# Later loading of one weight half, column-tiled bias product and shared moments in the prologue of a two-layer graph kernel

## Chip, cores and metric

The kernel runs as one program on one core of one Trainium2 chip. The metric is the device time of one execution in microseconds (us). The engines that matter here are TensorE (PE, matmuls and transposes), VectorE (DVE), ScalarE (ACT), GpSimd (POOL) and the DMA engines, which SyncE (SP) and ACT feed. Each engine works through its own instructions in order, so that an instruction that waits holds up all that stands behind it.

## What is computed

There are 1250 nodes with 512 features each and 40,000 edges with a source, a target and a row of 512 attributes. Cut to what matters:

```
h  = relu(layernorm(x))
msg = (h[src] + edge_attr) @ Wm.T + bm           # 40000 x 512
agg = segment_sum(msg, dst) / max(degree, 1)
upd = concat(h, agg) @ Wu.T + bu                 # Wu is 512 x 1024
x  = x + layernorm(h + gelu(upd)) * gamma + beta
h  = relu(layernorm(x))
x  = x + (relu(((1 + eps) * h + segment_sum(h[src], dst)) @ W1 + b1) @ W2 + b2) + h
```

## The kernel before

The edge attributes are 82 MB and are read once. They come in 79 groups of 512 edges (1 MB each), and one loop, `for n in range(NG)`, stands on every engine; "group n" below is one turn of it. Three kinds of work lie in a group on PE:

- `sums(n)` (line 1091; line 1099 from group 59 on) multiplies a one-hot matrix of targets (`oneD`) with the group's rows (`ea`) in 4 slots. ACT copies the result out (`packed_copy`, line 481), PE transposes it (`turn`, line 1119), ACT copies that out (`turned_copy`, line 487, two buffers `turned_sums`), and POOL adds it to `aggT` (`add_sums_of`, line 422, two additions for a group). Since there are two buffers, `turned_copy(n)` waits from n = 2 on for POOL's additions of group n - 2 (semaphore `early_step`).
- `counts(m)` (line 1110) multiplies one-hot matrices of sources and keys (`oneS`, `oneK`, line 675 on DVE), and DVE adds the result to the table of counts `A16` in two halves (line 696). The counts run ahead: groups 0, 3, 6, ... have two, the others one, until all are done in group 58 (`FULL`). `counts(m)` waits for the additions of counts m - 2.
- One piece of other work may stand at the end of a group (`ASIDE`): a transpose of four 128x128 blocks of h (`T_AT`, line 1132), the first quarter of a product h times Wu's first half (`U_AT`, line 1137; the other three quarters stand in later groups), or, in groups 0 and 1, a product of the prologue. They write PSUM banks 6 and 7 in turn, and each waits until the one two places before it has been copied out (`bank_free`).

Ahead of the loop stands a prologue. Wu is 512 x 1024; its second half (`Wu2T`) is needed for the products CT = Wm.T times Wu2.T (line 1054), its first half (`Wu1T`) only for the quarters of line 1137. PE transposes all eight block columns (line 1036), makes product 0, transposes the tables of indices (line 1061), and makes products 1 and 2. Product 3 stands in group 0, and the product of the bias bm with Wu2 in group 1, as four matmuls whose stationary operand `bmB` is bm broadcast to 128 columns.

x's moments: DVE takes `bn_stats` of seven of ten row blocks before the loop and of three in group 0 (line 777), aggregates them (line 782) and writes `ve` (line 784). POOL raises it to the power -1/2 (line 408). This instruction stands on POOL ahead of all its additions of line 422. DVE makes `nb0` of it in group 2 (line 827), and ACT writes h block by block from group 2 on (`H0_AT`, line 492).

The DMA queue of SP holds, in order: indices, Wu's first half, Wm, edge groups 0 and 1, x, bm, edge groups 2 and 3, bu; then edge group n + 4 after `sums(n)`. ACT's queue holds Wu's second half in two parts. After group 58, `Hh` takes h's high part (line 504), `A16` is converted in pieces (line 515), and from group 60 on PE multiplies them (lines 1190 and 1191).

## Time and profile before

| | us |
|---|---|
| median of 3 runs (lowest to highest) | 490.38 (489.9 to 492.35) |
| profiled execution, its own time | 489.93 |
| its span, first to last instruction | 488.1 |
| PE busy | 472.6, 97% of the span |
| DVE, ACT, POOL busy | 269.4, 158.0, 122.2 |

The span is cut into stretches by reading when `sums(n)` starts: `sums(0)` at 25.91 us, `sums(5)` at 43.70, `sums(8)` at 51.40, `sums(48)` at 158.82 and `sums(60)` at 188.68. Idle time of an engine costs something only where another one waits for it in the end; PE is the engine to watch.

### The profile page before, as it was taken

The numbers are of one execution on the slowest core, as the hardware profiler recorded it, in microseconds if no ns is written. First come the engines' busy times: TensorE is split into PE (matmuls) and PEld (weight loads), VectorE is DVE, ScalarE is ACT, GpSimd is POOL, SyncE is SP. The second block draws the span as 40 slices with busy tenths as digits, with TensorE's granted clock in tenths as the row PEclk, the third lists the DMA queues.
The fourth block names the chain that finished last, engine by engine and source line by source line (L and its number), as shares of the span: only waits on it lengthen the run. The fifth ranks groups of instructions, "written<-read, shape, count | busy, mean of one in ns | idle before, by whom it ended". The sixth has DMA issues, their size and how long they took to land.

```text
span 488.1 us, 9290 instructions
## 1 busy us (share of the span) xinstructions
PE 472.6 (97%) x3275; PEld 277.4 (57%) x3275; DVE 269.4 (55%) x621; ACT 158.0 (32%) x291; POOL 122.2 (25%) x183
## 2 busy tenths in 40 slices
PE   4999999999999999999999999899999999999997
PEld 3545555555555446776766655699744449444442
DVE  4789878787878887977857699923000000011011
ACT  6726633332333327411047287620012123000000
POOL 4005433444343432000001113349990000000000
PEclk9899999999999999999999999999999999999999
DMA  8998999999999999999430111040130000010111
GB/s 297 381 351 282 410 389 395 398 407 401 396 391 397 397 401 405 401 339 299 147 109 24 43 30 53 0 173 1 45 128 1 0 0 1 21 43 21 44 43 38
DMA packets 31641, 98.92 MB, mean 203 GB/s; under 512 B 3593, under 2 KB 4617, under 8 KB 31595
## 3 DMA queue, kind: packets, MB, share of 16 engines
q1 hardware_dynamic: 30458, 97.27, 53.1%
q10 hardware_dynamic: 1136, 1.05, 0.7%
q8 instruction: 27, 0.44, 0.4%
q14 instruction: 20, 0.16, 0.1%
HBM read 95.76 MB, written 2.56 MB: 201 GB/s over the span
## 4 chain that ended last, share of the span: by engine, by line
PE 81%; DVE 10%; DMA 4%; issue 3%; SPq 1%; POOL 1%; DVEq 0%; POOLq 0%
PE ps L1355 14%; PE ps L1340 14%; PE ps L1091 10%; PE ps L1137 7%; PE ps L1110 6%; PE ps L1190 6%; PE ps L1191 5%; PE ps L1287 4%; PE ps L1099 4%; DMA X<-in_x_dram 4%; PE ps L1119 4%; PE ps L1263 3%; PE ps L1264 3%; DVE A L696 2%; DVE stats L777 1%
## 5 line engine op out<-in xcount | busy, mean ns | idle before, releaser
L422 POOL TENSOR_TENSOR aggT<-turned_sums,aggT 128x88 f32 x118 | 62.5, 530 | 88.1 <-ACT turned_sums L487 74.8
L1025 DVE TENSOR_TENSOR U<-ps,U 128x512 f32<-128x512 f32 (+1 forms) x10 | 6.9, 693 | 128.5 <-PE ps L1355 128.5
L696 DVE TENSOR_TENSOR A<-ps,A 128x220 f32 x158 | 60.7, 384 | 28.6 <-PE ps L1110 18.0
L1355 PE MATMUL ps<-W2s,hid 128*128 128x512 f32 (+1 forms) x160 | 68.8, 592 | 0.0
L1340 PE MATMUL ps<-aggT,W1s 128*128 (+1 forms) x192 | 67.3, 513 | 0.0
L1091 PE MATMUL ps<-ea,oneD 128*22 128x256 f32 x944 | 62.7, 383 | 0.0
L1340 PEld LDWEIGHTS ps<-aggT,W1s 128*128 128x128 f32 x192 | 36.4, 190 | 30.7 <-issue 30.6
L1355 PEld LDWEIGHTS ps<-W2s,hid 128*128 128x128 f32 (+1 forms) x160 | 30.0, 188 | 38.2 <-issue 38.2
L481 ACT COPY packed_sums<-ps 128x256 f32<-128x256 f32 x59 | 22.0, 372 | 90.4 <-PE ps L1091 90.4
L1091 PEld LDWEIGHTS ps<-ea,oneD 128*22 128x22 f32 x944 | 22.6, 101 | 46.5 <-issue 21.7
L1263 PE MATMUL ps<-AR,Hh 128*128 128x256 f32 (+2 forms) x160 | 44.0, 311 | 0.7 <-DVE Hl L992 0.7
L1264 PE MATMUL ps<-AR,Hl 128*128 128x256 f32 (+2 forms) x160 | 43.0, 306 | 0.0
L1110 PE MATMUL ps<-oneK,oneS 128*128 128x220 bf16 x316 | 41.2, 260 | 1.7 <-DVE A L696 1.5
L675 DVE TENSOR_TENSOR oneK<-iotaP,P_key 128x1760 bf16<-128x1760 bf16 (+1 forms) x40 | 42.3, 1057 | 0.0
L1137 PE MATMUL ps<-Wu1T,U 128*128 128x512 f32 x80 | 41.3, 598 | 0.0
L605 ACT ACTIVATE hid<-ps,b1C 128x512 f32 (+1 forms) x24 | 14.6, 608 | 77.7 <-PE ps L1340 77.7
L432 POOL TENSOR_TENSOR rs<-ve,mhalf 128x1 f32<-128x1 f32 x10 | 8.3, 829 | 113.1 <-DVE ve L957 113.1
L1287 PE MATMUL ps<-CT,aggT 128*128 128x512 f32 x80 | 35.7, 592 | 0.0
L1190 PE MATMUL ps<-ARc,Hh 128*128 128x512 f32 x80 | 33.8, 423 | 0.0
L1110 PEld LDWEIGHTS ps<-oneK,oneS 128*128 128x128 bf16 x316 | 29.7, 97 | 5.0 <-DVE oneK L675 2.2
L1263 PEld LDWEIGHTS ps<-AR,Hh 128*128 128x128 f32 x160 | 30.2, 189 | 2.7 <-DVE Hl L992 1.1
L1191 PE MATMUL ps<-ARc,Hl 128*128 128x512 f32 x80 | 31.6, 394 | 0.0
(133 smaller groups left out, 642.7 us busy)
## 6 DMA issues: line engine op xcount, KB each, us to landing
ea<-in_edge_attr_dram SPq DMA_DIRECT2D x78, 1024.0 KB, 7.8
X<-in_x_dram SPq DMA_DIRECT2D x1, 2304.0 KB
xt<-in_x_dram SPq DMA_DIRECT2D x9, 256.0 KB, 3.5
out_dram<-U SPq DMA_DIRECT2D x9, 256.0 KB
W1s<-in_L_gnn_W_dram SPq DMA_DIRECT2D x1, 2048.0 KB, 9.1
W2s<-in_L_gnn_W_dram SPq DMA_DIRECT2D x1, 2048.0 KB, 8.5
WuN<-in_L_gnn_Wu_dram ACTq DMA_DIRECT2D x2, 512.0 KB, 4.4
WuN<-in_L_gnn_Wu_dram SPq DMA_DIRECT2D x1, 1024.0 KB, 6.8
```

Source lines behind the costliest of these rows:

```text
L422: nc.gpsimd.tensor_tensor(cols, sums, cols, ALU.add).then_inc(early_step, 1)
L696: V.tensor_tensor(cols, ps[:, 4 + m % 2, half * KW:(half + 1) * KW].rearrange("p (h w) -> p h w", w=W), cols, ALU.add).then_inc(add_step, 1)
L1091: last = T.matmul(to.rearrange("p (c d) -> p c d", c=2), oneD[h][:, g * 2 + j, :], data, start=j == 0, stop=j == 1)
L1110: last = T.matmul(ps[:, 4 + m % 2, (j // 2) * KW:(j // 2 + 1) * KW], sources[:, j // 2, :, j % 2], keys[:, j // 2, :, j % 2], start=j % 2 ...
L1137: quarter = T.matmul(ps[:, ASIDE_BANK["u1", b], :], U[:, b, f * P:(f + 1) * P], Wu1T[:, f, :], start=f == 0, stop=f == FC - 1)
L1190: T.matmul(to, Hh[:, c, rows], here, start=c == 0 and (q < 2 or f % 2 == 0), stop=False)
L1191: last = T.matmul(to, Hl[:, c, rows], here, start=False, stop=c == NT - 1 and (q < 2 or f % 2 == 1))
L1263: T.matmul(to, Hh[:, b, rows], AR[:, b, start:start + cols], start=b == 0 and (cols == 512 or f % 2 == 0), stop=False)
L1264: last = T.matmul(to, Hl[:, b, rows], AR[:, b, start:start + cols], start=False, stop=b == NT - 1 and (cols == 512 or f % 2 == 1))
L1287: last = T.matmul(ps[:, 2 + b % 2, :], aggT[:, f, b * P:(b + 1) * P], CT[:, f, :], start=f == 0, stop=f == FC - 1)
L1340: last = T.matmul(ps[:, CHUNK_BANK[k % 4], 0:cols], W1s[:, f, k * P:(k + 1) * P], aggT[:, f, bass.ds(start, cols)], start=f == 0, stop=f = ...
L1355: last = T.matmul(ps[0:rows, 6 + b % 2, :], hid[:, k, b * P:b * P + rows], W2s[:, k, :], start=k == 0, stop=k == KC - 1)
```

## The change

- The DMA of Wu's first half (now its own tile `Wu1N`) goes behind x in SP's queue; its four transposes move from the prologue into groups 2 to 5, with their copies on ACT.
- The prologue's order on PE is: four transposes of Wu's second half, products 0 and 1, the tables of indices, product 2. Product 3 is cut in two halves, in groups 0 and 1.
- The bias product is made in groups 57 and 58: four matmuls that write 32 rows each (column tiles, line `bias_parts`), a copy, and one matmul with a matrix of ones that adds the four. `Wu2T` and `WmN` have to live until then, so they lie in `Hh`, and `high_h0(0)` waits for the end of the bias product.
- DVE takes the moments of row blocks 0 to 4 only, in groups 0 and 1. Blocks 5 to 9 are ACT's: five ACTIVATEs that write the row sum with `accum_out` in group 0, five that square x minus the mean with `accum_out` in group 2. DVE makes the means in group 1 and `ve` in group 3; `nb0` moves to group 4, and h's blocks (`H0_AT`) from groups 2 to 11 to groups 5 to 14.
- h's transposes move from groups 4, 5, 6, 9, 15, ... 45 to 6, 7, 9, 15, ... 45, 48; the quarters start in group 8, not 7, and one of them stands in group 54.
- The least indices of targets (`offs`) are written and sent first, and the zeroing of `aggT` on ACT stands ahead of `A16`'s second half; the sum of uncovered edges is taken in group 6.

```diff
-    MOMENTS = 7
+    MOMENTS = [(0, 3), (3, 5)]
+    BY_ACT = slice(5, NT)
-    H0_AT = list(range(2, 2 + NT))
-    T_AT = [4, 5, 6] + list(range(9, 9 + 6 * (NT - 3), 6))
-    QUARTERS = [n for n in range(7, FULL) if len(COUNTS[n]) == 1 or (n % 6 == 0 and 6 < n < 48)]
+    LATE_PRODUCT_AT = [0, 1]
+    WU1_AT = [2, 3, 4, 5]
+    BIAS_PRODUCT_AT = [FULL - 1, FULL]
+    H0_AT = list(range(5, 5 + NT))
+    T_AT = [6, 7, 9] + list(range(15, 15 + 6 * (NT - 4), 6)) + [48]
+    QUARTERS = [n for n in range(8, FULL) if len(COUNTS[n]) == 1 or (n % 6 == 0 and n not in T_AT)]
...
-            sp.dma_start(WuN[:, :, 0:D], Wu[:, 0:D].rearrange("(o p) i -> p o i", p=P)).then_inc(wu1_in, 16)
             sp.dma_start(WmN[:], Wm.rearrange("(m p) i -> p m i", p=P)).then_inc(wm_in, 16)
...
                     sp.dma_start(X[0:TAIL, NT - 1, :], x[(NT - 1) * P:N, :]).then_inc(x_in, 16)
+                    sp.dma_start(Wu1N[:], Wu[:, 0:D].rearrange("(o p) i -> p o i", p=P)).then_inc(wu1_in, 16)
...
+            def sums_of_x():
+                act.wait_ge(x_in, 32)
+                for b in range(*BY_ACT.indices(NT)):
+                    nc.scalar.activation(U[:, b, :], X[:, b, :], ACT.Copy, accum_out=stats[:, b, 0:1]).then_inc(x_sums, 1)
+
+            def squares_of_x():
+                act.wait_ge(x_means, 1)
+                for b in range(*BY_ACT.indices(NT)):
+                    nc.scalar.activation(U[:, b, :], X[:, b, :], ACT.Square, bias=stats[:, b, 1:2], accum_out=stats[:, b, 2:3]).then_inc(x_squares, 1)
+
             def high_h0(b):
+                if b == 0:
+                    act.wait_ge(ct_mm, FC + 1)
...
                 if 0 < n <= EARLY:
                     turned_copy(n - 1)
+                if n == 0:
+                    sums_of_x()
+                if n - 1 == LATE_PRODUCT_AT[1]:
+                    product_out(EAGER)
+                if n == 2:
+                    squares_of_x()
                 if n - 1 in ASIDE:
                     kind, k = ASIDE[n - 1]
-                    if kind == "product" and k < FC:
-                        product_out(k)
+                    if kind == "wu1":
+                        wuT(FC + k)
...
-            dve.wait_ge(x_in, 32)
-            x_moments(0, MOMENTS)
             dve.wait_ge(offs_in, 16)
...
-                if n == 0:
-                    x_moments(MOMENTS, NT)
+                if n < len(MOMENTS):
+                    if n == 0:
+                        dve.wait_ge(x_in, 32)
+                    x_moments(*MOMENTS[n])
+                if n == 1:
+                    x_means_by_act()
+                if n == 3:
                     x_variances()
-                if n == 2:
+                if n == 6:
+                    uncovered_edges()
+                if n == 4:
                     dve.wait_ge(rs_ready, 1)
...
+            def bias_parts():
+                pe.wait_ge(bmB_done, 3)
                 for m in range(FC):
-                    last = T.matmul(ps[:, ASIDE_BANK["product", k], :], WmN[:, m, k * P:(k + 1) * P] if k < FC else bmB[:, m, :], Wu2T[:, m, :],
-                                    start=m == 0, stop=m == FC - 1)
-                last.then_inc(ct_mm, 1)
+                    last = T.matmul(ps[m * QUAD:(m + 1) * QUAD, ASIDE_BANK["product", FC], :], bmB[:, m, :], Wu2T[:, m, :], start=True, stop=True)
+                last.then_inc(bm_mm, 1)
+
+            def bias_product():
+                pe.wait_ge(bm_out, 1)
+                T.matmul(ps[:, ASIDE_BANK["product", FC], :], onesP[:], bm_parts[:], start=True, stop=True).then_inc(ct_mm, 1)
...
+                elif kind == "wu1":
+                    pe.wait_ge(wuT_done, FC + k + 1)
```

The last two lines are in `bank_free`: a transpose of Wu's first half that stands two places behind another one waits until ACT has copied that one out.

On PE the prologue stood like this before (block columns of Wu transposed, a product, the tables, two products, the first group):

```order
L1036 MATMUL ps<-ident,WuN 128x128 x32
L1054 MATMUL ps<-Wu2T,WmN 128x512 x4
L1061 MATMUL ps<-ident,g_srel 128x79 x4
L1061 MATMUL ps<-ident,g_key 128x79 x4
L1061 MATMUL ps<-ident,g_lo_f 128x79 x4
L1054 MATMUL ps<-Wu2T,WmN 128x512 x8
L1091 MATMUL ps<-ea_68,oneD_72 22x256 x8
```

and stands like this now:

```order
L1098 MATMUL ps<-ident,Wu2N 128x128 x16
L1112 MATMUL ps<-Wu2T,WmN 128x512 x8
L1129 MATMUL ps<-ident,g_srel 128x79 x4
L1129 MATMUL ps<-ident,g_key 128x79 x4
L1129 MATMUL ps<-ident,g_lo_f 128x79 x4
L1112 MATMUL ps<-Wu2T,WmN 128x512 x4
L1159 MATMUL ps<-ea_71,oneD_75 22x256 x8
```

Sixteen transposes have left the head, and one product has moved ahead of the tables.

On ACT groups 0 to 3 stood like this before, from the copies of products 1 and 2 on (`packed_sums` and `turned_sums` are the copies of the sums, `CT` that of a product, `X` is h):

```order
L462 COPY CT<-ps 128x512 x2
L481 COPY packed_sums_75<-ps 128x256
L481 COPY packed_sums_76<-ps 128x256
L487 COPY turned_sums_77<-ps 128x256
L462 COPY CT<-ps 128x512
L481 COPY packed_sums_75<-ps 128x256
L487 COPY turned_sums_78<-ps 128x256
L492 ACTIVATE X<-X,nb_150,rs_149 128x512
L481 COPY packed_sums_76<-ps 128x256
L487 COPY turned_sums_77<-ps 128x256
```

and now, from the first `packed_copy` on:

```order
L501 COPY packed_sums_78<-ps 128x256
L529 ACTIVATE U,stats<-X 128x512 x5
L501 COPY packed_sums_79<-ps 128x256
L507 COPY turned_sums_80<-ps 128x256
L501 COPY packed_sums_78<-ps 128x256
L507 COPY turned_sums_81<-ps 128x256
L481 COPY CT<-ps 128x512
L534 ACTIVATE U,stats<-X,stats 128x512 x5
L501 COPY packed_sums_79<-ps 128x256
L507 COPY turned_sums_80<-ps 128x256
L475 COPY Wu1T<-ps 128x512
L501 COPY packed_sums_78<-ps 128x256
```

The third `turned_sums` copy is `turned_copy(2)`; behind it now stands the copy of Wu's first transposed block column.

On DVE the statistics stood before the first count and in group 0 (`oneD` for group 3 opens group 1):

```order
L777 BN_STATS stats<-X 128x6 x3
L782 BN_AGGR mv<-stats 128x2 x10
L784 TENSOR_SCALAR ve<-mv 128x10
L665 TENSOR_TENSOR oneD_72<-iotaF,T_srel 128x88
```

and now two batches stand in groups 0 and 1, with the whole of group 1's count between them:

```order
L823 BN_STATS stats<-X 128x6 x3
L711 TENSOR_TENSOR oneD_75<-iotaF,T_srel 128x88
L742 REGISTER_ALU
L742 ISA
L742 TENSOR_TENSOR A_53<-ps,A_53 128x10x22
L721 TENSOR_TENSOR oneK_82<-iotaP,P_key 128x1760
L730 TENSOR_LOAD offrow
L742 ISA
L742 TENSOR_TENSOR A_53<-ps,A_53 128x10x22
L823 BN_STATS stats<-X 128x6 x2
L827 TENSOR_SCALAR stats<-stats 128x5
L828 TENSOR_SCALAR mv<-stats 128x5
```

`ve` is now written behind counts 0 to 5, where it stood behind counts 0 and 1.

## Rows read from the trace of the kernel before

**Rows 1.** The page, busy time by engine.

```profile
PE 472.6 (97%) x3275; PEld 277.4 (57%) x3275; DVE 269.4 (55%) x621; ACT 158.0 (32%) x291; POOL 122.2 (25%) x183
```

**Rows 2.** Windows: length, busy time of five engines, granted clock, DMA share, GB/s.

```profile
7.99:11.41 3.42, 1.50 (x12) 1.03 (x11) 3.21 (x7) 1.61 (x4) 0.00 (x0) 1.00 1.05 391
11.41:14.82 3.41, 3.41 (x10) 2.33 (x11) 3.20 (x7) 1.55 (x3) 0.00 (x0) 0.50 1.03 407
...
51.40:158.82 107.42, 107.31 (x1028) 55.60 (x1027) 85.82 (x201) 39.85 (x100) 44.12 (x81) 1.00 1.02 398
```

**Rows 3.** Timeline of PE, prologue: start, length, engine, line, what.

```profile
4.65 3.69 PE L1036 MATMUL ps<-ident,WuN 128*128 128x128 f32 x16 [4.65 <-DMA WuN<-in_L_gnn_Wu_dram]
10.02 1.09 PE L1036 MATMUL ps<-ident,WuN 128*128 128x128 f32 x8 [1.68 <-DMA WuN<-in_L_gnn_Wu_dram]
...
17.52 0.59 PE L1061 MATMUL ps<-ident,g_srel 79*128 79x79 f32 x4
```

**Rows 4.** Timeline of PE, `sums(5)` and `sums(8)`.

```profile
43.70 1.06 PE L1091 MATMUL ps<-ea,oneD 128*22 128x256 f32 x16
...
51.40 0.84 PE L1091 MATMUL ps<-ea,oneD 128*22 128x256 f32 x12
```

**Rows 5.** The chain that ended last, one group's parts: start, us, what.

```profile
48.40 0.44 PE ps L1132 x4
...
49.83 0.37 PE ps L1119 x2
...
50.60 0.87 PE ps L1137 x2
...
54.10 0.99 PE ps L1091 x16
...
58.04 0.39 PE ps L1110 x4
```

**Rows 6.** Timeline of DVE, 23 to 45 us.

```profile
23.61 0.68 DVE L675 TENSOR_TENSOR oneS<-iotaP,P_lo 128x1024 bf16<-128x1024 bf16 x1
...
30.85 0.39 DVE L696 TENSOR_TENSOR A<-ps,A 128x220 f32 x1 [0.84 <-DVE nunc L790]
...
34.00 1.87 DVE L777 BATCH_NORM_STATS2 stats<-X 128x6 f32<-128x512 f32 x3
35.90 0.77 DVE L782 BATCH_NORM_AGGREGATE mv<-stats 128x2 f32<-128x6 f32 x10
...
40.81 0.23 DVE L665 TENSOR_TENSOR oneD<-iotaF,T_srel 128x88 f32<-128x88 f32 x1
...
44.11 0.24 DVE L665 TENSOR_TENSOR oneD<-iotaF,T_srel 128x88 f32<-128x88 f32 x1
```

**Rows 7.** Timeline of POOL: the power, then the second addition of group 0.

```profile
37.04 1.98 POOL L408 TENSOR_TENSOR rs<-ve,mhalf 128x10 f32<-128x10 f32 x1 [10.56 <-DVE ve L784]
...
39.59 0.56 POOL L422 TENSOR_TENSOR aggT<-turned_sums,aggT 128x88 f32 x1 [0.23 <-POOL aggT L422]
```

**Rows 8.** Timeline of ACT: h's first block, `turned_copy(2)`, a copy out of PSUM.

```profile
40.32 0.81 ACT L492 ACTIVATE X<-X,nb,rs 128x512 f32<-128x512 f32 x1 [1.89 <-DVE nb L827]
...
41.29 0.37 ACT L487 COPY turned_sums<-ps 128x256 f32<-128x256 f32 x1
...
45.44 0.59 ACT L496 COPY U<-ps 128x512 f32<-128x512 f32 x1
```

**Rows 9.** DMA issues at 180 to 182 us, edge group 60: KB, us to landing.

```profile
ea<-in_edge_attr_dram SPq DMA_DIRECT2D x1, 1024.0 KB, 7.8
```

**Rows 10.** Waits of PE, 150 to 192 us: total, times, longest.

```profile
PE ps L1110 <- DVE A L696: 0.8, 3, 0.3
```

**Rows 11.** Timeline of PE, `sums(60)` and the first piece.

```profile
188.68 1.07 PE L1099 MATMUL ps<-ea,oneD 128*22 128x128 f32 x32 [1.03 <-DVE oneD L665]
189.69 0.50 PE L1190 MATMUL ps<-ARc,Hh 128*128 128x512 f32 x1
```

**Rows 12.** Timeline of ACT, the first piece converted.

```profile
188.48 0.62 ACT L515 CAST ARc<-A 128x512 fp32r<-128x512 uint16 x1
```

More of the change, by code:

```diff
@@ L24 @@
 COUNT_MAX = 4096
-PREP_SPANS = 4
+PREP_FIRSTS = 3
 PREP_KEYS = 11
@@ L457, in wuT @@
                 act.wait_ge(wuT_mm, n + 1)
-                nc.scalar.copy(Wu1T[:, k, :] if k < FC else Wu2T[:, k - FC, :], ps[:, 6 + n % 2, :]).then_inc(wuT_done, 1)
+                if k < FC:
+                    nc.scalar.copy(Wu1T[:, k, :], ps[:, ASIDE_BANK["wu1", k], :]).then_inc(wuT_done, 1)
+                else:
+                    nc.scalar.copy(Wu2T[:, k - FC, :], ps[:, 6 + n % 2, :]).then_inc(wuT_done, 1)
             def product_out(k):
@@ L470, in _ @@
             zero_counts(0, HB // 2)
[L471 removed]
+            for n in range(FC):
                 wuT(n)
[L473 to L475 removed]
+            offs_row = offrow[:].rearrange("a (g k) -> a g k", k=4)
+            act.wait_ge(prep, PREP_FIRSTS)
+            act.dma_start(offs_row[:, :, 0:2], offs[0:NG, 0:2]).then_inc(offs_in, 16)
+            nc.scalar.activation(aggT[:], iotaF[:, 0:1].rearrange("p (a b) -> p a b", a=1).broadcast_to([P, FC, SWD]), ACT.Copy, scale=0.0).then_inc(sums_zero, 1)
             def packed_copy(n):
@@ L1035, in transpose_wu @@
                 for o in range(FC):
-                    last = T.transpose(ps[:, 6 + n % 2, o * P:(o + 1) * P], WuN[:, o, k * P:(k + 1) * P], ident[:])
+                    if k < FC:
+                        last = T.transpose(ps[:, ASIDE_BANK["wu1", k], o * P:(o + 1) * P], Wu1N[:, o, k * P:(k + 1) * P], ident[:])
+                    else:
+                        last = T.transpose(ps[:, 6 + n % 2, o * P:(o + 1) * P], Wu2N[:, o, (k - FC) * P:(k - FC + 1) * P], ident[:])
                 last.then_inc(wuT_mm, 1)
-            for n in range(2 * FC):
+            for n in range(FC):
                 if n == 0 or n == FC // 2:
                     pe.wait_ge(wu2_in[n // (FC // 2)], 16)
-                if n == FC:
-                    pe.wait_ge(wu1_in, 16)
                 if n >= 2:
@@ L1046, in _, with product @@
                 transpose_wu(n)
-            def product(k):
-                if k < 2:
-                    pe.wait_ge(wuT_done, 2 * FC - 1 + k)
-                if k == FC:
-                    pe.wait_ge(bmB_done, 1)
-                for m in range(FC):
-                    last = T.matmul(ps[:, ASIDE_BANK["product", k], :], WmN[:, m, k * P:(k + 1) * P] if k < FC else bmB[:, m, :], Wu2T[:, m, :],
-                                    start=m == 0, stop=m == FC - 1)
-                last.then_inc(ct_mm, 1)
+            def product(k, first=0, count=FC):
+                if k == 0:
+                    pe.wait_ge(wuT_done, FC)
+                for m in range(first, first + count):
+                    last = T.matmul(ps[:, ASIDE_BANK["product", k], :], WmN[:, m, k * P:(k + 1) * P], Wu2T[:, m, :], start=m == 0, stop=m == FC - 1)
+                if first + count == FC:
+                    last.then_inc(ct_mm, 1)
+            def bias_parts():
+                pe.wait_ge(bmB_done, 3)
+                for m in range(FC):
+                    last = T.matmul(ps[m * QUAD:(m + 1) * QUAD, ASIDE_BANK["product", FC], :], bmB[:, m, :], Wu2T[:, m, :], start=True, stop=True)
[3 more added lines that the diff above has]
+                T.matmul(ps[:, ASIDE_BANK["product", FC], :], onesP[:], bm_parts[:], start=True, stop=True).then_inc(ct_mm, 1)
             def transpose_indices(mine, to, ready):
@@ L1065, in _ @@
             product(0)
+            product(1)
             pe.wait_ge(prep, PREP_KEYS)
@@ L1068, in _ @@
                 transpose_indices(mine, 2 + q, idxT_mm)
-            for k in range(1, EAGER):
-                if k >= 2:
-                    pe.wait_ge(ct_done, k - 1)
+            for k in range(2, EAGER):
+                pe.wait_ge(ct_done, k - 1)
                 product(k)
@@ L1155, in aside @@
                     bank_free(ASIDE_ORDER[order - 2])
-                if kind == "product":
-                    product(k)
+                if kind == "product" and k < FC:
+                    product(k, 0, FC // 2)
+                elif kind == "product":
+                    bias_parts()
                 elif kind == "transpose":
                     transpose_h0(k)
+                elif kind == "wu1":
+                    if k == 0:
+                        pe.wait_ge(wu1_in, 16)
+                    transpose_wu(FC + k)
                 else:
@@ L1205, in _ @@
                             u1(b, f)
+                if n == LATE_PRODUCT_AT[1]:
+                    product(EAGER, FC // 2, FC // 2)
+                if n == BIAS_PRODUCT_AT[1]:
+                    bias_product()
                 if n in ASIDE:
```

77 lines of the change are left out of this document (50 added, 27 removed).

## Prediction

> **What bounds the kernel now.** I read the page first: PE is busy for 472.6 of 488.1 us, no other engine for more than 55% [rows 1]. So only what PE does or waits for can count. Then the windows: between `sums(8)` and `sums(48)` PE is busy 107.31 of 107.42 us, at the full clock, while the DMA share is 1.02 [rows 2]. PE sets the pace there and the DMA engines have nothing to spare. The chain of waits gives the parts of a group: sums 0.99, turn 0.37, one count 0.39, and 0.44 for a transpose of four blocks or 0.87 for one 128x512 matmul [rows 5]. A group with one count and one such matmul is 2.62 us.
>
> Since PE is full from 51.4 us on, a change in the prologue is worth the shift that it gives `sums(8)`, plus what it adds to or takes from PE later. `sums(5)` starts at 43.70 and `sums(8)` at 51.40 [rows 4].
>
> **Step 1, the head of PE.** Now eight block columns are transposed, and the last four could start only when Wu's first half had landed, at 10.02 [rows 3]. Wm takes that place in the queue and is as large (1 MB), so product 0 starts at about 10.0. Products 0 and 1 are 8 matmuls of 0.87 us [rows 5], 7.0 us, so the tables of indices come at 17.0 at full clock. They came at 17.52 [rows 3].
>
> The clock decides the rest. From 7.99 to 11.41 PE was busy for 1.50 of 3.42 us, and in the next 3.41 us the granted clock was 0.50, which is 1.2 instead of 2.4 GHz [rows 2]. After the change PE waits for Wm just as long (8.3 to 10.0), but is busy from 10.0 on, some 1.8 of 3.4 us. No row shows such a share before a fall or before none; it is nearer to the 1.50 that was followed by the low clock than to the full stretches that were not. I take the fall as likelier. It costs half of 3.41 us, 1.7: the tables come at 18.7, 1.2 us late; without the fall they come 0.5 early.
>
> The Trainium skill ("TensorE: Matmul & The Clock Gate", Part 4: PE-mode transpose) says that transposes don't count as PE being busy for the clock. By that rule the clock would stay up, for products stand where transposes stood. The trace speaks against the rule: the first 16 transposes took 3.69 us, 0.23 each, the next 8 took 1.09, 0.14 each [rows 3], so the clock had risen behind nothing but transposes.
>
> **Step 2, the head's gain.** Of PE's work before `sums(0)` the 16 later transposes go. From the tables at 17.52 to `sums(0)` at 25.91 (the start given with the profile) it was 8.4 us, of which one product of 3.5 has moved ahead. So `sums(0)` starts at 18.7 + 4.9 = 23.6 with the low clock, 2.3 earlier, and at 21.9 without. The bias product (four matmuls, 3.5 us) leaves group 1, and four transposes of 0.44 come in groups 2 to 5. Up to group 4 PE thus gets some 4 us ahead.
>
> **Step 3, what takes it back.** Here is the wait on which the forecast rests. `turned_copy(2)` needs POOL's additions of group 0, and these stand behind POOL's power, which needs `ve`. Before, `ve` was written behind two counts; now behind six. DVE's chain after its last `oneS` of the prologue, from its own rows [rows 6]: 0.84 until the first A; counts 0 and 1, 3.15 (30.85 to 34.00); three `bn_stats` 1.9 (34.00 to 35.90); counts 2 and 3 with their `oneD`, 3.3 (as 40.81 to 44.11); two `bn_stats` 1.25 and two small operations, each under `oneD`'s 0.24, together 0.25; counts 4 and 5, 3.3; five of ten aggregations 0.39; two small operations with their waits 0.3. Sum 14.7 us. It began at 24.2 (`oneS` at 23.61, the next operation can start 0.6 behind it); now it begins at 25.4 with the low clock, 23.7 without. `ve` is written at 40.1 or 38.4; it was about 36.9, since POOL's power started at 37.04 [rows 7]. So it comes 3.2 (1.5) us later, although the seven `bn_stats` have left the space before the counts.
>
> From there: power 0.15 + 1.98, the two additions 1.13 (39.02 to 40.15) [rows 7], `turned_copy(2)`, whose successor starts 0.3 behind it, and the copy of Wu's first block column, 0.59 [rows 8]. Two places further, in group 4, PE may write that bank again: at 44.4 (42.7). The transpose is 0.44, so `sums(5)` starts at 44.8 (43.1), 1.1 later (0.6 earlier) than 43.70. What was late before is not late: the edge groups have landed while PE stands, and DVE catches up too.
>
> Between `sums(5)` and `sums(8)` PE has a transpose of 0.44 in group 7 where it had 0.87. So `sums(8)` starts 0.7 later with the low clock and 1.0 earlier without it.
>
> ACT's ten operations with `accum_out` are not in the rows. The nearest is h's ACTIVATE with a bias, 0.81 [rows 8]; the lower bound is the 0.59 of a plain copy. The squares start behind the means (25.4 + 0.84 + 3.15 + 1.9, half of 3.3 and some more for count 2, 1.5, so 34.7) and take 5 x 0.8, until 38.7; DVE asks for them ahead of its last two operations, at 39.8. So they are hidden up to about 1.0 each, and each 0.1 above that costs 0.5 us.
>
> **Step 4, what comes back later.** The transpose in group 48 is new: there PE had only two counts, and waited for DVE's additions a little later, three times in this stretch, 0.8 us by the view of waits [rows 10]; so it fills a wait, 0. The quarter in group 54 costs 0.87, of which such a wait covers 0.44: 0.43. The bias parts are four matmuls in four column tiles. The sums run so: 8 matmuls of 256 columns in 0.99 us [rows 5], where eight in a row would need four times as much. Half as many of 512 columns: 0.9. The matmul with ones is 0.87 in group 58. At group 60 PE waited 1.03 us; the view names DVE, but edge group 60, issued between 180 and 182 us, needed 7.8 us to land, and `sums(60)` began at 188.68 [rows 9, 11], so it was the landing. With PE later this wait goes, yet the first piece of ACT, ready at 189.10 [rows 12], would have held PE to 189.2 where it began its piece at 189.69 [rows 11]: 0.5 back. ACT's piece stands behind `high_h0(0)`, which stands behind the bias product, but moves no more than PE does. Together 0.43 + 0.9 + 0.87 - 0.5 = 1.7. Bounds: 1.2 if the whole 1.0 comes back, 3.1 if nothing is covered and nothing comes back.
>
> **The sum.** Low clock 0.7 + 1.7 = 2.4; full clock -1.0 + 1.7 = 0.7. The profiled execution took 489.93 us, 0.45 below the median of the three runs; 489.93 + 2.4 = 492.3, and 490.6.
>
> **Rivals.**
> - The clock stays at 2.4 GHz: 490.6, chance 0.25. For it: PE is busier ahead of 11.4 us than before. Against it: the wait in front is the same.
> - The gain of the head arrives: `ve` comes by 36 us, so that ACT has Wu's block column out before PE needs the bank. Then `sums(8)` starts some 4.4 us earlier and 1.7 come back: 487.2, chance 0.09. For it: DVE idles here and there in rows that I add up. Against it: six counts in place of two ahead of `ve`, each pair over 3 us. This lies on the other side of no change; it decides from `ve` at about 37 us on downwards.
> - ACT's sums and squares take over 1.0 us each; at 1.4 the squares hold `ve` by 2.0 us more: 494.3, chance 0.10.
> - The column tiles run one after another, 3.5 for 0.9: 494.9, chance 0.05. The sums' rows speak against it.
> - The extra copies on DVE in group 59 (the bias product's) or a late edge group: within a microsecond, in the ranges.
>
> **Numbers.** The main case, low clock and the wait at group 4, has 0.42; its own range is 491.2 to 493.8. 0.09 is left for what none of these says. About 0.5% (2.45 us) is what a measurement of this kernel can tell from no change: faster is below 487.9, slower above 492.8. A third of the main case lies above, with the two slow rivals 0.30. Faster is the second rival, 0.09. The rest is 0.61. The range reaches from the full-clock case less 1.2 to the slow rivals, 489.4 to 494.6.
>
> **What would show it.** Right: the tables of indices at about 18.7 (17.0 if the clock stays); `sums(0)` near 23.6; DVE's `ve` near 40; POOL's power behind it; PE idle for 4 to 5 us in group 4, released by ACT's copy of `Wu1T`; `sums(5)` near 44.8; ACT's five operations near 0.8 each; bias parts 0.9; no wait at `sums(60)`. Wrong: no wait over 1 us in group 4, or `sums(8)` before 49; or a granted clock of 1.00 throughout 11 to 15 us, which moves the time to 490.6.

## The result and the profile after

The changed kernel takes 494.45 us (median of 10 runs, 492.33 to 495.86), the kernel before on the same chip 490.40 (489.9 to 492.35). The ratio is 1.0070, 95% interval 1.0050 to 1.0089: slower by 0.7%. A second measurement of the changed kernel (e9 below) gave 494.47 and 1.0081 (1.0060 to 1.0102). One run of e8 (604.76 us, mean granted clock 0.755) and one of the kernel before beside e7 and e10 (502.94 us, 0.943) were slow ones, and the ratios leave them out.

The profiled execution took 495.69 us, 5.76 more than the one of before. PE's busy time has hardly grown against [rows 1]:

```profile
PE 473.6 (96%) x3277; PEld 277.7 (56%) x3277; DVE 266.5 (54%) x614; ACT 165.7 (34%) x312; POOL 120.0 (24%) x185
```

So the question is where PE stood. Its waits up to 60 us (line waited for, total, times, longest):

```profile
PE ps L1098 <- DMA Wu2N<-in_L_gnn_Wu_dram: 4.9, 1, 4.9
PE ps L1096 <- ACT Wu1T L475: 4.8, 1, 4.8
PE ps L1112 <- DMA WmN<-in_L_gnn_Wm_dram: 2.3, 1, 2.3
```

The first is the wait for the first weights, which both kernels have at their start. The second is the forecast wait: PE stands in group 4 for ACT's copy of Wu's first half. The timeline of PE gives the course (start, length, line, what, idle time before and its releaser); L1096 are transposes of Wu's first half, L1112 the products, L1129 the tables, L1159 and L1167 `sums`, L1119 and L1124 the bias product, L1268 the first piece:

```profile
10.99 9.70 PE L1112 MATMUL ps<-Wu2T,WmN 128*128 128x512 f32 x16 [2.35 <-DMA WmN<-in_L_gnn_Wm_dram]
20.52 0.59 PE L1129 MATMUL ps<-ident,g_srel 79*128 79x79 f32 x4
...
25.48 0.85 PE L1159 MATMUL ps<-ea,oneD 128*22 128x256 f32 x12
...
44.90 1.12 PE L1096 MATMUL ps<-ident,Wu1N 128*128 128x128 f32 x4 [4.80 <-ACT Wu1T L475]
45.95 1.92 PE L1159 MATMUL ps<-ea,oneD 128*22 128x256 f32 x16
...
54.92 1.06 PE L1159 MATMUL ps<-ea,oneD 128*22 128x256 f32 x16
...
188.63 1.06 PE L1119 MATMUL ps<-Wu2T,bmB 128*32 128x512 f32 x8
189.51 1.05 PE L1159 MATMUL ps<-ea,oneD 128*22 128x256 f32 x16
...
191.16 1.03 PE L1124 MATMUL ps<-bm_parts,onesP 128*128 128x512 f32 x2
192.13 1.07 PE L1167 MATMUL ps<-ea,oneD 128*22 128x128 f32 x32
...
193.50 1.07 PE L1167 MATMUL ps<-ea,oneD 128*22 128x128 f32 x32
195.27 0.47 PE L1268 MATMUL ps<-ARc,Hh 128*128 128x512 f32 x1 [0.70 <-DVE Hl L776]
...
197.51 0.74 PE L1167 MATMUL ps<-ea,oneD 128*22 128x128 f32 x20
```

`sums(5)` starts at 45.95 and lasts 1.92 us, where it starts at 43.70 and lasts 1.06 in [rows 4]; `sums(8)` starts at 54.92 for 51.40. The reader should notice that the loss doesn't end with the wait: from `sums(5)` to `sums(8)` it grows by another 1.27 us. The windows show why (length, busy times, granted clock, DMA share, GB/s):

```profile
44.90:48.30 3.40, 3.40 (x23) 1.69 (x24) 0.00 (x0) 1.45 (x4) 1.65 (x5) 0.50 0.02 6
48.30:51.70 3.40, 3.40 (x31) 2.22 (x30) 1.66 (x4) 1.97 (x6) 0.76 (x2) 0.70 0.77 255
...
54.92:162.55 107.63, 107.47 (x1027) 55.60 (x1027) 86.87 (x206) 42.91 (x105) 43.21 (x81) 1.00 1.02 390
```

Behind the wait the granted clock is 0.50, which is 1.2 GHz, for the whole of the first window, and the second window has 0.70 on average; what PE does there at the low clock takes twice its time (the sums' 16 matmuls last 1.92 us where they last 1.06). The chain that releases PE is read from three engines, DVE first, then POOL, then ACT:

```profile
40.66 0.17 DVE L837 TENSOR_SCALAR ve<-mv 128x10 f32<-128x10 f32 x1
```

```profile
40.98 1.97 POOL L424 TENSOR_TENSOR rs<-ve,mhalf 128x10 f32<-128x10 f32 x1 [13.64 <-DVE ve L837]
42.93 0.37 POOL L438 TENSOR_TENSOR aggT<-turned_sums,aggT 128x88 f32 x1
43.53 0.37 POOL L438 TENSOR_TENSOR aggT<-turned_sums,aggT 128x88 f32 x1 [0.23 <-POOL aggT L438]
```

```profile
30.56 0.37 ACT L507 COPY turned_sums<-ps 128x256 f32<-128x256 f32 x1
...
38.17 0.70 ACT L534 ACTIVATE U<-X,stats 128x512 f32<-128x512 f32 x1
38.78 0.18 ACT L534 ACTIVATION_READ_ACCUMULATOR U<-X,stats 128x1 f32 x1
...
43.99 0.37 ACT L507 COPY turned_sums<-ps 128x256 f32<-128x256 f32 x1 [4.77 <-POOL aggT L438]
44.26 0.59 ACT L475 COPY Wu1T<-ps 128x512 f32<-128x512 f32 x1
```

`ve` is written, POOL's power runs, the two additions of group 0 follow, ACT had been waiting for them for 4.77 us, copies `turned_sums` and then Wu's block, and PE goes on at 44.90. POOL had waited 13.64 us for `ve`, though the sums of group 0 lay ready for its additions from 31 us on (ACT's copy at 30.56).

The sum of the difference, by the starts of `sums` in the two profiled executions: 3.52 us up to `sums(8)`, 0.21 up to `sums(48)` (107.63 for 107.42), 1.32 up to `sums(58)` (parts and quarter), 0.72 up to `sums(61)`. That is 5.77 of 5.76: nothing else counts. This execution was 1.24 us above the median, though, and the one of before 0.47 below its own. The profiled execution of e9 (the same kernel, 494.61 us) is nearer to the median: its `sums(5)` starts at 44.86, `sums(8)` at 53.92 and `sums(61)` at 196.48, so of its 4.68 us 2.52 are lost up to `sums(8)` and 2.22 behind it.

### The profile page after: what moved, and what is told of

Its sections match the earlier page's. It is cut to its first block, busy times and chain, and to the rows that moved or that the text cites. A ratio compares the mean times of both kernels' runs of the same rounds, so it can differ in the third digit from the quotient of the medians.

```text
span 493.9 us, 9317 instructions
## 1 busy us (share of the span) xinstructions
PE 473.6 (96%) x3277; PEld 277.7 (56%) x3277; DVE 266.5 (54%) x614; ACT 165.7 (34%) x312; POOL 120.0 (24%) x185
## 3 DMA queue, kind: packets, MB, share of 16 engines
q10 hardware_dynamic: 1216, 1.05, 0.7%
## 4 chain that ended last, share of the span: by engine, by line
PE 85%; DVE 8%; issue 3%; DMA 2%; POOL 1%; DVEq 0%; ACT 0%; SPq 0%; POOLq 0%; ACTq 0%
PE ps L1437 14%; PE ps L1422 14%; PE ps L1159 11%; PE ps L1207 7%; PE ps L1178 6%; PE ps L1268 5%; PE ps L1269 4%; PE ps L1369 4%; PE ps L1187 4%; PE ps L1167 4%; PE ps L1345 3%; PE ps L1112 3%; PE ps L1346 3%; DMA WmN<-in_L_gnn_Wm_dram 2%; DVE A L742 1%
## 5 line engine op out<-in xcount | busy, mean ns | idle before, releaser
L438 POOL TENSOR_TENSOR aggT<-turned_sums,aggT 128x88 f32 x118 | 60.3, 511 | 92.3 <-ACT turned_sums L507 79.0
L1159 PE MATMUL ps<-ea,oneD 128*22 128x256 f32 x944 | 63.6, 388 | 0.0
L1159 PEld LDWEIGHTS ps<-ea,oneD 128*22 128x22 f32 x944 | 22.9, 102 | 47.6 <-issue 22.3
L1268 PE MATMUL ps<-ARc,Hh 128*128 128x512 f32 x80 | 33.8, 422 | 0.7 <-DVE Hl L776 0.7
```

The lines of the kernel that those rows point to most:

```text
L438: nc.gpsimd.tensor_tensor(cols, sums, cols, ALU.add).then_inc(early_step, 1)
L1159: last = T.matmul(to.rearrange("p (c d) -> p c d", c=2), oneD[h][:, g * 2 + j, :], data, start=j == 0, stop=j == 1)
L1268: T.matmul(to, Hh[:, c, rows], here, start=c == 0 and (q < 2 or f % 2 == 0), stop=False)
```

## The experiments

All runs below were timed against the kernel before on the same chip beside them: its median was 491.63 us for e1 to e4, 490.46 for e5, e6, e8 and e9, and 491.65 for e7 and e10. The times of before lie at two levels (see the last section), so its median moves with how many runs fall on each. From one such group to another it moved by up to 1.25 us, so the ratios to before are a surer measure than differences of medians from different groups.

**e1: the power behind three groups of additions.** It takes the disputed wait away and leaves all else.

```diff
-            pool.wait_ge(consts, 3)
-            pool.wait_ge(ve_ready, 1)
-            nc.gpsimd.tensor_tensor(rs0[:], ve[:], mhalf[:], ALU.pow).then_inc(rs_ready, 1)
...
             for n in range(EARLY):
+                if n == 3:
+                    pool.wait_ge(consts, 3)
+                    pool.wait_ge(ve_ready, 1)
+                    nc.gpsimd.tensor_tensor(rs0[:], ve[:], mhalf[:], ALU.pow).then_inc(rs_ready, 1)
                 add_sums_of(n)
```

> Edit: POOL's power for x's layernorm stands behind its additions of groups 0 to 2 instead of ahead of all of them; nothing else differs from the changed kernel. Theory W (the changed kernel loses because turned_copy(2) waits for additions that stand behind that power, and because the 4.8 us of idle PE then pull the granted clock down): PE's wait in group 4 falls from 4.80 us to under 1 us, the clock stays at full level from 16 us on, sums(8) starts at 47 to 49 us instead of 54.9, and since the edge groups cannot land faster than one in 2.56 us, PE waits for some of them between groups 17 and 35, 2 to 3 us in all. Time about 489, 5 to 6 us under the changed kernel. Rival theory D (VectorE's six counts ahead of ve and the later Wm with the low clock in the prologue are the loss, POOL only shows it): the wait moves to VectorE's additions or to its nb0, sums(8) stays behind 52 us, time 493 or more.

Measured: 488.78 us (487.58 to 489.54), ratio 0.9948 (0.9929 to 0.9967). One edit takes 5.7 us off the median of the changed kernel and turns the change into a gain of 0.5% over before. POOL's timeline shows the additions of groups 0 to 2 ahead of the power now (the last of them is the first row), and the power runs for as long as before but no long wait of PE follows from it:

```profile
38.65 0.34 POOL L434 TENSOR_TENSOR aggT<-turned_sums,aggT 128x88 f32 x1 [0.20 <-POOL aggT L434]
39.38 1.98 POOL L442 TENSOR_TENSOR rs<-ve,mhalf 128x10 f32<-128x10 f32 x1 [0.39 <-DVE ve L837]
```

In PE's timeline `sums(5)` starts at 38.90, 7.05 us earlier than in the changed kernel. 1.71 us of that are the start of this one execution (`sums(0)` at 23.77 for 25.48), which the edit doesn't touch; from `sums(0)` to `sums(5)` it is 15.13 us for 20.47, so 5.34 are the edit's, and from there to `sums(8)` another 1.54 (7.43 for 8.97). The row of the wait for Wu's block is gone, and what is left of waits in groups 0 to 8 is 1 us in all:

```profile
PE ps L1178 <- DVE A L742: 0.6, 2, 0.3
PE ps L1187 <- ACT packed_sums L501: 0.4, 1, 0.4
```

So the theory of the wait holds, and the rival that put the loss on DVE's six counts and the head falls. Of the 2 to 3 us of waits for edges that were expected before group 35 only 0.9 came. Against the changed kernel's profiled execution `sums(8)` is 8.6 us earlier (46.33), `sums(61)` 7.8 (189.71) and the end 6.3. The windows name both losses: up to `sums(30)` this kernel takes 59.77 us, where the changed one takes 58.98 (54.92 to 113.90), with the DMA share at 1.02, and at 215 us the clock falls once, which costs some 1.5 us and is taken up in the last section.

```profile
46.33:106.10 59.77, 58.86 (x565) 30.62 (x564) 47.88 (x115) 26.28 (x62) 24.48 (x45) 1.00 1.02 396
...
214.70:218.10 3.40, 3.40 (x16) 2.23 (x18) 1.50 (x7) 0.16 (x1) 0.00 (x0) 0.50 0.69 275
```

**e2: the wait filled with useless work.** The wait stays in time, but PE is busy in it.

```diff
+                if (kind, k) == ("wu1", 2):
+                    for f in range(9):
+                        T.matmul(ps[:, 1, 256:512], ident[:], Wu1N[:, f % FC, 0:256], start=True, stop=True)
```

> Edit: nine extra 128x256 matmuls with no use stand on PE in group 4, just ahead of the third transpose of Wu's first half, where PE waited 4.80 us; they write unused columns. The wait itself is not removed. Theory W with the clock as its second part: the idle time falls to about 1 us, the granted clock is not lowered at 43 to 50 us, sums(5) starts at the same 46 us or 0.2 earlier, but sums(8) starts 1.7 to 2.2 us earlier (near 53), time 2 us under the changed kernel, 492.5. Rival (the low clock behind the wait is hidden by VectorE's counts): no change in time, within 0.5 us.

Measured: 493.87 us (493.02 to 494.64), ratio 1.0055 (1.0034 to 1.0077). PE's timeline where it goes on, with `sums(5)`; then the window behind that point, and a later one:

```profile
44.87 0.66 PE L1096 MATMUL ps<-ident,Wu1N 128*128 128x128 f32 x4 [0.90 <-ACT Wu1T L475]
45.45 1.06 PE L1159 MATMUL ps<-ea,oneD 128*22 128x256 f32 x16
```

```profile
44.40:47.80 3.40, 2.93 (x34) 1.95 (x38) 0.31 (x2) 2.77 (x8) 1.92 (x7) 1.00 0.12 31
...
221.20:224.60 3.40, 3.40 (x36) 2.09 (x35) 0.89 (x3) 0.62 (x1) 0.00 (x0) 0.50 0.29 116
```

The clock stays at 1.00, and `sums(8)` starts at 52.42, 2.50 us earlier than in the changed kernel, though the block column comes as late (PE goes on at 44.87 for 44.90). From `sums(5)` at 45.45 to `sums(8)` it is 6.97 us for 8.97: the low clock costs 2.0 us there, and 0.5 in the transpose ahead of `sums(5)`. In this profiled execution 1.5 us were lost again at 221 us, where the clock fell once. The median gives only 0.6 us back where 2 had been expected. Five of the six runs have the same mean granted clock as this execution (0.997), so they may have lost the 1.5 us as well; that isn't shown. The cost of the clock is shown in place; what of it reaches the median isn't settled by this run.

**e3: the head filled.** Five useless matmuls in PE's wait for Wm.

```diff
+            for _ in range(5):
+                T.matmul(ps[:, 5, 0:P], ident[:], ident[:], start=True, stop=True)
             pe.wait_ge(wm_in, 16)
             product(0)
```

> Edit: five extra 128x128 matmuls with no use stand on PE between the last transpose of the prologue and product 0, in PE's wait of 2.3 us for Wm. Theory W: the clock rises earlier in the prologue, the tables of indices come 1 to 2.6 us earlier than 20.5, so VectorE's chain up to ve and the wait in group 4 end that much earlier; the length of the wait stays near 4.8 us. Time 1 to 2.5 us under the changed kernel. Rival (the head is not on the path, only the number of counts ahead of ve is): sums(5) stays at 45.9 and the wait grows by what the head gained.

Measured: 493.25 us (492.52 to 493.79), ratio 1.0041 (1.0027 to 1.0056), 1.2 us less than the changed kernel. The eight matmuls of the two products take 7.13 us in place of 9.70:

```profile
10.58 7.13 PE L1112 MATMUL ps<-Wu2T,WmN 128*128 128x512 f32 x16 [0.22 <-DMA WmN<-in_L_gnn_Wm_dram]
```

The tables come at 17.55 for 20.52, and the writing of `ve` ends at 38.0 for 40.8, but the wait for Wu's block is still 4.9 us, for everything on both sides of it moved together. `sums(8)` starts at 52.04, 2.9 us earlier than in the changed kernel's first profile and 1.9 earlier than in its second (e9, tables at 19.43). The low clock of the start thus costs 1.2 us in the medians, and 2.6 or 1.7 by the two products (9.70 in the first profile, 8.83 in e9).

**e4: without the bias product.** The parts and the matmul with ones are left out, so this kernel leaves bm out of the result.

```diff
-                for m in range(FC):
-                    last = T.matmul(ps[m * QUAD:(m + 1) * QUAD, ASIDE_BANK["product", FC], :], bmB[:, m, :], Wu2T[:, m, :], start=True, stop=True)
-                last.then_inc(bm_mm, 1)
+                T.sem_inc(bm_mm, 1)
...
-                T.matmul(ps[:, ASIDE_BANK["product", FC], :], onesP[:], bm_parts[:], start=True, stop=True).then_inc(ct_mm, 1)
+                T.sem_inc(ct_mm, 1)
```

> Edit: the four matmuls of the bias parts in group 57 and the matmul with ones in group 58 are left out (the bias term of the first layer is left out with them, its copies stay), to price the late bias product. The price of its two pieces by the trace is 0.88 and 0.97 us, and PE waits 0.70 us for VectorE at the first piece in group 60. If these lie on PE's path: 1.9 to 2.5 us under the changed kernel, near 492.3, with the wait at the first piece 0 to 0.7. Rival (PE has slack for them before group 60, since VectorE or the edge groups pace it there): under 1 us.

Measured: 494.41 us (492.42 to 496.06), ratio 1.0059 (1.0039 to 1.0078); the medians see nothing. The profiled execution says more: `sums(8)` starts at 53.48 and `sums(61)` at 194.74, 141.26 us apart for 142.59 in the changed kernel. So the bias product costs 1.3 us, and not the 1.74 by which it lengthens the way from `sums(57)` to `sums(59)` (5.64 us for 3.90), because without it a wait comes back, which stood in [rows 11] and is nowhere in the changed kernel:

```profile
191.34 1.07 PE L1165 MATMUL ps<-ea,oneD 128*22 128x128 f32 x32 [0.97 <-DVE oneD L711]
```

That price is read from one pair of executions; the medians neither confirm nor exclude it.

**e9: the changed kernel once more**, unaltered, as measure for e5, e6 and e8.

> The changed kernel, not altered, as the measure for the three runs beside it. All theories expect what it gave: a wait of 4.8 us of TensorE in group 4 for ScalarE's copy of the third transposed block of Wu1, the clock at its lower level behind it, sums(8) near 55, and 494.5 us (493.5 to 495.5).

Measured: 494.47 us (494.24 to 496.31), and again PE waits 4.8 us for ACT's copy of `Wu1T`. The point where PE goes on, `sums(5)` and `sums(8)`:

```profile
43.81 1.11 PE L1096 MATMUL ps<-ident,Wu1N 128*128 128x128 f32 x4 [4.80 <-ACT Wu1T L475]
44.86 1.92 PE L1159 MATMUL ps<-ea,oneD 128*22 128x256 f32 x16
...
53.92 1.06 PE L1159 MATMUL ps<-ea,oneD 128*22 128x256 f32 x16
```

Here the records show the low clock of the start too, where the first profile reads 1.00 although its matmuls take up to twice their time; the window behind the wait for Wm:

```profile
11.41:14.82 3.41, 3.41 (x6) 1.28 (x5) 3.21 (x7) 3.38 (x1) 0.00 (x0) 0.57 1.02 414
```

**e6: the moments undone.** All ten row blocks by DVE as before, seven ahead of the counts, `ve` in group 0.

```diff
-                if n == 0:
-                    sums_of_x()
...
-                if n == 2:
-                    squares_of_x()
...
+            dve.wait_ge(x_in, 32)
+            x_moments(0, 7)
             dve.wait_ge(offs_in, 16)
...
-                if n < len(MOMENTS):
-                    if n == 0:
-                        dve.wait_ge(x_in, 32)
-                    x_moments(*MOMENTS[n])
-                if n == 1:
-                    x_means_by_act()
-                if n == 3:
+                if n == 0:
+                    x_moments(7, NT)
+                    x_variances()
```

> The changed kernel with one part undone: all ten of x's moments by VectorE as before (seven bn_stats pairs ahead of the counts, three in group 0, and the variance there), none by ScalarE; the three early products and the late bias stay. Theory: the wait in group 4 comes from the variance being asked behind six counts, so here the variance is written near 36.5, GpSimd's power ends near 38.5, the wait for the copy of Wu1 falls from 4.8 to under 1 us, the clock does not fall behind it, and sums(8) stands near 51.5: 491 us (490 to 492). Rival: the seven moments ahead of the counts push VectorE's chain by as much as was won, the tables start 1 to 2 us later, and it is 492.5 us (491.8 to 493.5). Second rival, the wait comes of the products in front of the groups and not of the variance: the wait stays over 3 us and it is 494 us or more.

Measured: 491.62 us (490.51 to 495.12), ratio 1.0021 (1.0002 to 1.0040), 2.9 us less than the changed kernel. `ve` is written at 35.95 and there is no wait for Wu's block at all; `sums(5)` starts at 42.54, `sums(8)` at 49.77. In its place the counts of group 1 wait for DVE, which is at the moments, and the clock falls behind that wait too (0.52 in the window behind it): the two matmuls of product 3 take 3.13 us where they take 1.83 in the changed kernel (27.27 to 29.09 and 30.75 to 32.58):

```profile
31.73 0.89 PE L1169 MATMUL ps<-oneK,oneS 128*128 128x220 bf16 x4 [2.63 <-DVE A L738]
32.42 3.20 PE L1103 MATMUL ps<-Wu2T,WmN 128*128 128x512 f32 x4
35.55 1.06 PE L1150 MATMUL ps<-ea,oneD 128*22 128x256 f32 x16
```

```profile
31.73:35.20 3.47, 3.47 (x8) 1.61 (x8) 3.30 (x9) 0.00 (x0) 0.00 (x0) 0.52 1.03 411
```

So the moved moments, with the place of `ve` behind six counts, are what makes the wait in group 4; the second rival, which put it on the products ahead of the groups, falls. The move isn't useless: it relieves the counts of group 1. What spoils it is where `ve` and the power stand.

**e8: the power behind group 0's additions in the kernel before.**

```diff
-            pool.wait_ge(consts, 3)
-            pool.wait_ge(ve_ready, 1)
-            nc.gpsimd.tensor_tensor(rs0[:], ve[:], mhalf[:], ALU.pow).then_inc(rs_ready, 1)
...
             for n in range(EARLY):
+                if n == 1:
+                    pool.wait_ge(consts, 3)
+                    pool.wait_ge(ve_ready, 1)
+                    nc.gpsimd.tensor_tensor(rs0[:], ve[:], mhalf[:], ALU.pow).then_inc(rs_ready, 1)
                 add_sums_of(n)
```

> The kernel before with GpSimd's power behind the additions of group 0, the edit that gave the changed kernel 5.7 us. Theory: in the kernel before nothing waits long for these additions, since the variance is written before they are asked, so the edit is worth nothing there: the median stays within 0.3% of before (489.9 to 492.6), with sums(5) within 0.5 us of 43.7. Rival: the power's 2 us stand in the path of before too, and it gets 1.5 to 2 us faster (489 us), in which case the edit and not the changed order is what won over before.

Measured: 490.87 us (489.90 to 492.69 and the one run of 604.76, without which the median is 490.32), ratio 1.0006 (0.9989 to 1.0024); `sums(5)` starts at 44.15. The power cost nothing that can be measured in the kernel before, so what e1 gains over before doesn't come from moving the power alone. The edit is not quite e1's: the power stands behind one group's additions here, behind three there.

**e7: the head filled in the kernel before.**

```diff
                 if n == FC:
+                    T.matmul(ps[:, 5, 0:256], ident[:], WuN[:, 0, D:D + 256], start=True, stop=True)
                     pe.wait_ge(wu1_in, 16)
```

> The kernel before with one useless 128x256 matmul ahead of the wait for Wu's first half, in a wait of 1.6 us that the low clock of the start follows. Theory: work in that wait keeps the clock from staying low behind it, the products in front of the groups run at the higher level and sums(0) comes about 1 us earlier, but groups 0 to 2 wait there for VectorE's counts, so that nothing of it is left at sums(5) (43.7 within 0.4): 490.5 us (489.8 to 492.3), no change. Rival: the start is on the path in before too, and it gets 0.8 to 1.5 us faster, 489.3 us.

Measured: 491.04 us (489.77 to 491.94), ratio 0.9991 (0.9976 to 1.0006): no difference. The tables come at 16.50 for 17.52, and the microsecond is gone at `sums(5)` (43.96), spent in longer waits for the additions of the counts, 2.0 us for the 0.7 of before:

```profile
PE ps L1111 <- DVE A L696: 2.0, 3, 1.3
```

**e5: e1 and the filled head together.** (The two diffs of e1 and e3.)

> The changed kernel with GpSimd's power behind the additions of groups 0 to 2 (which by itself gave 488.8 us) and five useless 128x128 matmuls ahead of the first product, in TensorE's wait for Wm (which by itself took 1.2 us off). If the low clock at the start is still on the path when the group-4 wait is gone, the chain of groups begins 1.3 us earlier (sums(0) at 22.5 for 23.8) and the kernel takes 487.6 us (487.0 to 488.3). If the transfers of the edges set the pace once the groups run ahead (their slack in the run with the power moved was down to 0.1 to 0.4 us near group 25), the earlier start is lost there in waits of the sums for their tables, and it is 488.8 us again (488.3 to 489.5).

Measured: 489.27 us (487.80 to 489.99), ratio 0.9959 (0.9944 to 0.9975), no better than e1. The start is earlier as foreseen (`sums(0)` at 22.50, `sums(8)` at 45.48, 0.85 before e1's), but `sums(30)` starts at 106.08 for 106.10. Two windows (to `sums(8)` and from there to `sums(30)`), and the waits whose releaser the profile doesn't name:

```profile
22.50:45.48 22.98, 21.89 (x220) 12.68 (x220) 21.12 (x54) 16.99 (x45) 8.19 (x15) 1.00 1.03 399
45.48:106.08 60.60, 59.05 (x564) 30.88 (x564) 47.86 (x115) 25.95 (x61) 24.33 (x45) 1.00 1.02 395
```

```profile
PE ps L1161 <- issue: 1.5, 2, 1.0
```

L1161 is `sums`, and the waits stand ahead of groups 21 (0.51 us) and 25 (1.00). The DMA view gives what the view of waits doesn't: the transfer of group 21 was issued at 70.69 us and needed 10.3 to land, that of group 25 at 82.17 and needed 10.7, so they landed at 81.0 and 92.9, and the sums start at 81.05 and 92.99. The row of the latter (KB, us to landing):

```profile
ea<-in_edge_attr_dram SPq DMA_DIRECT2D x1, 1024.0 KB, 10.7
```

The DMA share is 1.02 to 1.03 from the first group on. So the second case of the expectation holds: the transfers of the edges take back the earlier start. Directly ahead of these two transfers in the queue stand those of eps and gamma (0.5 and 256 KB); whether they add to the two waits was not tried.

**e10: the bias product where PE waits anyway.**

```diff
-    BIAS_PRODUCT_AT = [FULL - 1, FULL]
+    BIAS_PRODUCT_AT = [12, 13]
```

> The kernel with the power moved and the head filled, and the bias product's two parts moved from groups 57 and 58 to groups 12 and 13, where that kernel's sums wait for their edges anyway (3.8 us between two landings near groups 21 and 25). Theory: from sums(48) to sums(61) the kernel needs 33.0 to 33.6 us again for 35.0, and what the parts cost in groups 12 and 13 (2 to 2.7 us with a wait for ScalarE's copy) is nearly all taken up by those waits before group 30: 487.7 us (487.0 to 488.5) for 489.3. Rival: the cost of 2 us is only moved forward, because the transfers fall behind by as much when their buffers come free later: 489.3 us (488.6 to 490.0).

Measured: 488.57 us (486.92 to 489.01), ratio 0.9938 (0.9918 to 0.9959), the lowest median of all, though its interval overlaps those of e1 and e5. It is e5 with this one line. It lies between the two forecasts, 0.07 us above the range of the one and 0.03 below that of the other. The parts in group 12 wait 0.68 us for ACT and cost 0.88, the ones in group 13 cost 0.87:

```profile
60.20 1.06 PE L1119 MATMUL ps<-Wu2T,bmB 128*32 128x512 f32 x8 [0.68 <-ACT U L520]
61.08 1.05 PE L1161 MATMUL ps<-ea,oneD 128*22 128x256 f32 x16
...
62.73 1.03 PE L1124 MATMUL ps<-bm_parts,onesP 128*128 128x512 f32 x2
63.60 0.59 PE L1209 MATMUL ps<-Wu1T,U 128*128 128x512 f32 x1
```

From `sums(48)` to `sums(61)` it takes 33.24 us for the 34.96 of e1, as expected. From `sums(8)` to `sums(30)` it takes 61.33 us for the 60.60 of e5, so of the 2.43 us put into groups 12 and 13 (0.68 + 0.88 + 0.87) 1.7 were covered, which fits the waits for edges that e5 had there. `sums(8)` itself came 0.5 later than in e5 (45.97), with a slower start in this execution, and took part of the gain. At `sums(61)` it is 0.39 us ahead of e5 (189.30 for 189.69). The gain over e5 in the medians, 0.7 us between runs of different times, is no more than an indication.

## Why the prediction was right, and where it was short

The mechanism was right, and the sum was 2.1 us too small: 492.3 forecast, 494.45 measured. The forecast was less sure of the direction than its sum looks: 1.9 us over before is under the 2.45 that it called tellable, and it gave 0.61 to no tellable change and 0.30 to slower, which came. The time lies above the main case's own range (491.2 to 493.8). The full range holds it by 0.15 us, and that range reached so high only for two slow rivals, ACT's operations and the column tiles, and neither of them came. That is luck.

- **The wait of group 4** was forecast at 4 to 5 us, released by ACT's copy of `Wu1T`, through `ve`, the power and POOL's additions. It is 4.80 us, by that chain; e1 shows that it decides the sign, e6 that it comes from the moments.
- **The term that was wrong is the way from `sums(5)` to `sums(8)`.** It took the full clock as given ("in group 7 0.44 where it had 0.87", so 0.4 won). But PE stood for 4.80 us, longer than the 1.68 us in the head behind which the prediction had read a low clock [rows 3], and the clock fell behind it: 8.97 us (9.06 in e9) where the prediction had 7.27. The transpose ahead of `sums(5)` cost 0.5 more for the same reason. e2 keeps the clock up with useless work and gets 2.5 us back at `sums(8)`. The prediction weighed the clock in the head and forgot it in the wait that it had itself foretold. The Trainium skill ("TensorE: Matmul & The Clock Gate", Part 1, HAM oscillation) tells of a kernel whose waits for DMA let the clock gate drop, so that the next tile of work starts cold; the trace agrees here, with a wait for ACT (0.50 behind the wait of 4.80 us), and it should have been applied to the forecast wait as well.
- **The head.** The low clock was taken as likelier, and it came; only its size was small: 9.70 us for the two products in the profiled execution where 8.7 was forecast, 8.83 in e9. With Wm landing at 10.99 and not 10.0, the tables came at 20.52 for 18.7 (19.43 in e9), `sums(0)` at 25.48 for 23.6. The prediction had read Wm's landing off that of Wu's first half in the same place of the queue; it is 0.3 to 1.0 us later in the seven profiles in which PE waits for it (10.36 in e4 to 10.99).
- **DVE's chain up to `ve`** was mis-sized the other way. From the last `oneS` of the prologue to `ve` it took 14.2 us, in the first profile (26.61 to 40.83) and in e9 alike, where step 3 has 15.3 (0.6 and its sum of 14.7). So the tables came 1.8 us late but `ve` only 0.7 (40.83 for 40.1), and in e9 the tables were 0.7 late and `ve` came at 39.73. From `ve` to PE's going on it is 4.07 us; the prediction has 4.3, and its own terms add up to 4.15. That e9's `sums(5)` stands at 44.86, as good as the forecast 44.8, is therefore errors that cancel: PE goes on at 43.81, 0.6 us before the forecast 44.4, and its transposes take 1.05 us at the low clock for 0.44.
- **The rival "the gain of the head arrives"** didn't come: it needs `ve` at about 37, or the power elsewhere. With the power elsewhere e1 has `sums(8)` at 46.33 where this rival had 47.0, and 488.78 us for its 487.2, with 1.5 us lost at 215 us in the profiled execution.
- **ACT's sums and squares** each bring an ACTIVATION_READ_ACCUMULATOR of their own, of 0.18 to 0.19 us. From start to start a square takes 0.71 us and a sum 0.61, below the 0.8 that was assumed. The squares end at 38.96, before DVE reaches the aggregations at 40.13: hidden, as said.
- **The column tiles** run side by side: four matmuls of 512 columns in 0.88 us from start to start (188.63 to 189.51). The rival with 3.5 us is out.
- **Late in the loop** 1.7 was forecast, 2.25 measured. The quarter cost 0.44 (`sums(48)` to `sums(57)` is 23.94 us for 23.50) and the parts 0.88, for 0.43 and 0.9; the matmul with ones 0.86 (`sums(58)` to `sums(59)`, 2.62 for 1.76) for 0.87. The wait at `sums(60)` is gone as foreseen, 1.09 off, but the way from there to `sums(61)` is 0.95 longer (4.01 for 3.06) where the prediction had 0.5 come back: the first piece holds PE 0.70 us, now for DVE's `Hl`, and not for ACT. The prediction put the old wait at `sums(60)` down to the landing of edge group 60; in the trace of before that landing (issued at 180.8, 7.8 us) and the end of DVE's `oneD` (188.53) lie within 0.1 us of each other, so which of them it was stays open. The remaining 0.21 is spread over 107 us between groups 8 and 48, and is not explained.

With the fall of the clock (1.7 behind `sums(5)`, 0.5 ahead of it) the sum would have read 2.4 + 2.2 = 4.6, so 494.5 from the same profiled time. The difference of the profiled executions is 4.68 us with e9 and 5.76 with the first one, whose head took 1.1 us more (tables at 20.52 for 19.43).

## What to carry to other kernels

When work is taken from the front of an engine, ask at once what else its successors stand behind: here an independent power of 2 us in POOL's program order stood ahead of additions whose buffers two other engines needed, and moving it by three groups took more off (5.7 us) than the whole change had added (4 us). The wait on PE cost more than its length: behind 4.80 us of it the clock was at 0.50, and that cost 2.5 us more; a forecast that finds such a wait has to add a term for it. And a gain ahead of a stretch in which the DMA engines are full can end there, as in e5 (0.85 us at `sums(8)`, 0.02 at `sums(30)`); extra work put into such a stretch cost 0.73 of its 2.43 us in e10, though the gain in time is only indicated.
